# Layer 3 attention of a four-layer kernel: fp32 probabilities against values in four column tiles of the array, and row maxima taken bank by bank

## The reference, cut to what matters

```python
q = (q_input @ W_Q + b_Q)      # q_input is the layer norm of x: 16 x 56 x 128
k = (kv_input @ W_K + b_K)     # kv_input is ctx_1024: 16 x 1500 x 128
v = (kv_input @ W_V + b_V)
sim = einsum('bhqd,bhkd->bhqk', q, k) / sqrt(8)      # 16 heads of 8
sim = where(mask, finfo.min, sim)
attn = softmax(sim, axis=-1)
out = einsum('bhqk,bhkd->bhqd', attn, v)             # heads joined again
return out @ W_O + b_O
```

## Time and profile before

| | us |
|---|---|
| median of three executions | 1914.12 |
| lowest, highest | 1910.27, 1917.18 |
| profiled execution | 1911.53 |
| its span (first to last instruction) | 1909.8 |
| layer 3 attention, steady part of the span | 1222 to 1747 |

### The profile page before, as it was taken

The page is one execution under the profiler, slowest core; times in us unless marked ns, Lnnn a source line. Parts: engine busy times, 40 slices in busy tenths (PEclk is TensorE's granted clock), DMA queues, the critical chain, the costliest instruction groups (busy, mean ns, idle before and its releaser), DMA issues. The chain is left out here.

```text
span 1909.8 us, 31074 instructions
## 1 busy us (share of the span) xinstructions
PE 1628.9 (85%) x10638; PEld 1374.8 (72%) x10638; DVE 1356.4 (71%) x2304; ACT 932.8 (49%) x1353; POOL 706.8 (37%) x613
## 2 busy tenths in 40 slices
PE   3995686637999999999999957799999999996796
PEld 2994375436999999999999823577777777774795
DVE  5214544675888888888888633688888888883598
ACT  1331222224666666666666404466666666662332
POOL 0110000003333334334333001587877787873230
PEclk8897798668999999999999978799999999998798
DMA  2014496101111111111110001425344353520110
GB/s 54 23 44 112 115 237 118 33 1 33 34 59 40 32 32 48 49 32 32 32 56 8 3 3 49 112 68 118 80 100 98 84 114 81 115 54 3 56 45 21
DMA packets 97600, 116.02 MB, mean 61 GB/s; under 512 B 16785, under 2 KB 82882, under 8 KB 97538
## 3 DMA queue, kind: packets, MB, share of 16 engines
q1 hardware_dynamic: 97538, 115.23, 24.5%
HBM read 76.42 MB, written 0.46 MB: 40 GB/s over the span
## 5 line engine op out<-in xcount | busy, mean ns | idle before, releaser
L2295 POOL TENSOR_TENSOR l3att_PL<-l3att_P,l3att_PH 125x1120 fp32r<-125x1120 f32 x128 | 329.9, 2577 | 121.8 <-DVE l3att_PH L2376 61.3
L1728 ACT CAST l2att_PT<-PS 125x512 fp32r<-125x512 f32 x336 | 175.3, 595 | 221.3 <-PE PS L1667 221.3
L1768 DVE TENSOR_REDUCE l2att_neg<-PS 128x1 f32<-128x1500 f32 x112 | 192.7, 1720 | 76.8 <-PE PS L1660 76.8
L2197 ACT ACTIVATE l3att_P<-PS 125x1344 f32<-125x1344 f32 x128 | 165.4, 1292 | 136.9 <-PE PS L2077 134.9
L1774 DVE TENSOR_TENSOR l2att_PT<-PS,l2att_PT 125x512 fp32r<-125x512 f32 x336 | 210.1, 680 | 1.5 <-ACT l2att_PT L1728 1.5
L1667 PEld LDWEIGHTS PS<-all_ident,l_P 128*125 128x125 f32 x1344 | 163.5, 187 | 15.0 <-DVE l_P L1782 6.5
L1737 ACT ACTIVATE l_P<-PS,l2att_neg 128x1500 f32<-128x1500 f32 x112 | 171.0, 1527 | 3.9 <-DVE l2att_neg L1768 3.9
L1699 PE MATMUL PS<-l2att_PT,l_cc 125*128 125x256 f32 x576 | 170.5, 296 | 0.0
L1667 PE MATMUL PS<-all_ident,l_P 128*125 128x128 f32 x1344 | 165.4, 273 | 4.8 <-DVE l_P L1782 4.8
L1701 PE MATMUL PS<-l2att_PT,l_cc 125*128 125x256 f32 x576 | 162.5, 282 | 0.0
L1703 PE MATMUL PS<-l2att_PT,l_cc 125*128 125x256 f32 x576 | 162.4, 282 | 0.0
(11 more groups left out here) (526 smaller groups left out, 3755.3 us busy)
## 6 DMA issues: line engine op xcount, KB each, us to landing
l3att_KS<-l3att_kh SPq DMA_DIRECT2D x128, 187.5 KB, 4.0
l_QP<-in_ctxT SPq DMA_DIRECT2D x8, 1500.0 KB, 11.2
l_cT<-in_ctxT SPq DMA_DIRECT2D x16, 750.0 KB
l_c<-in_ctx SPq DMA_DIRECT2D x16, 750.0 KB
l3att_cT<-in_ctxT SPq DMA_DIRECT2D x16, 750.0 KB, 4.8
l3att_KS<-l3att_kl SPq DMA_DIRECT2D x64, 187.5 KB, 3.8
l_QP<-in_ctx SPq DMA_DIRECT2D x8, 1344.0 KB
l0f_w<-in_L_ffn_W SPq DMA_DIRECT2D x16, 256.0 KB, 3.1
```

What stands on the lines that cost most here:

```text
L1728: act.copy(PT[:, 4 * g:4 * g + 4, PLACE[u1], 0, :], PS[0:CHUNK, 3 * s1 + g, :].rearrange("k (c r) -> k c r", r=128)).then_inc(hi_in, 1)
L1768: v.tensor_reduce(neg[:, s:s + 1], E, XY_AXES, ALU.max, negate=True).then_inc(top_in, 1)
L2197: act.activation(P[s][:, PART * part:PART * part + PART, :].rearrange("p (i j) r -> p i (j r)", j=2), PS[0:CHUNK, 3:6, 0:2 * SET_ROWS], AC ...
L2295: g.tensor_tensor(PL[s][:, part, :, :], P[s][:, PART * part:PART * part + SPLIT, :], PH[s][:, part, :, :], ALU.subtract).then_inc(pl_in, 1)
```

## The change

The change is confined to layer 3's attention.

- `P` is no longer split. The casts to `PH`, the subtractions to `PL`, the fp32 copy `VF` of the values and their low part are gone. The values `VS` are fp32 with 9 columns for each head (`VCOLS` = 9: 8 features and a one).
- `values` issues, for each of 12 chunks, four fp32 matmuls, one for each head: weights 125 x 9, streamed 125 x 56, written to PSUM partitions 32h to 32h+8 of columns 0 to 55. Each head thus has its own 32 columns of the array. The blocks of four other pairs of heads are not computed.
- ACT copies the 128 x 56 result straight into `OC` (`outputs`). `OB` and the 64 extraction DMAs are gone. `OC`, `WOS`, `SEL` and `inv` have 128 partitions. DVE clears the 56 columns of banks 6 and 7 once at the start.
- The maxima are taken by the bank: six `tensor_reduce` of 500 keys for each group in place of two of 1500. The six row matmuls go to banks 0, 2, 0, 2, 0, 1 (`PLACES`), each waits for the maximum that read its bank before, and each raises `sr_ps`. Two small `tensor_reduce` (minimum over three) write `negs` and `negm` in place of the cast.
- The keys' projection and the matmul with `SEL` move from bank 2 to bank 1 (`SIDE`), the former to before `rows(2)`. The order on the PE becomes: rows 0 and 1, `values` of chunks 0 to 3, `maxima`, `project_keys`, the matmul with `SEL`, row 2, `project_values`, row 3, `turned(0)`, rows 4 and 5, `values` of chunks 4 to 11, `turned(1)`. ACT writes keys and values first, then exponential, output copy, exponential. DVE's list becomes: maxima 0 and 1, copy into `QB`, maximum 2, low keys, inverse, maxima 3 to 5, scaling of `OC`, the two minima, the subtraction.

The diff, cut to its core:

```diff
-VCOLS = 17
+VCOLS = 9
-SPLIT = PART - 1
+QUAD = 32
...
-            VS = [self.sb(ctx, f"VS{s}", [CHUNK, CHUNKS, SETS, SETS * VCOLS], F32R) for s in range(2)]
+            VS = [self.sb(ctx, f"VS{s}", [CHUNK, CHUNKS, SETS, SETS, VCOLS]) for s in range(2)]
...
-            PH, PL = ([self.sb(ctx, f"{n}{s}", [CHUNK, 2, SPLIT, SET_ROWS], F32R) for s in range(2)]
-                      for n in ("PH", "PL"))
...
-                            pe.wait_ge(vl_in, (n - 2) // SETS * BANKS + BANKS)
-                        parts = 1 if chunks[0] < PART else 2
-                        pe.wait_ge(pl_in, 2 * n - 4 + parts)
...
+                            if k % PART == 0 or k == chunks[0]:
+                                pe.wait_ge(p_in, 2 * n - 3 + k // PART)
+                            for h in range(SETS):
+                                mm = pe.matmul(PS[QUAD * h:QUAD * h + VCOLS, 6 + u % 2, 0:TOK],
+                                               VS[s][:, k, a, h, :], P[u % 2][:, k, TOK * h:TOK * h + TOK],
+                                               start=k == 0, stop=k == CHUNKS - 1)
...
+                    if now:
+                        rows((0, 1))
+                    if before:
                         values((0, 1, 2, 3))
...
+                    if now:
+                        rows((2,))
...
+                    if now:
+                        rows((3,))
+                    if then:
+                        turned(0)
+                    if now:
+                        rows((4, 5))
+                    if before:
+                        values((4, 5, 6, 7, 8, 9, 10, 11))
+                    if then:
+                        turned(1)
...
-                    def high_part():
-                        act.wait_ge(p_in, 2 * n - 1)
-                        act.copy(PH[s][:, 0, :, :], P[s][:, 0:SPLIT, :]).then_inc(ph_in, 1)
...
-                        act.copy(OB[:, a % SETS, :], PS[0:SETS * VCOLS, 6 + u % 2, 0:SET_ROWS]
+                        act.copy(OC[:, bass.ds((n - 2) // SETS, 1), a, :], PS[:, 6 + u % 2, 0:TOK].unsqueeze(1)
                                  ).then_inc(o_in, 1)
...
-                        for part in range(2):
-                            g.wait_ge(ph_in, 2 * n - 1 + part)
-                            g.tensor_tensor(PL[s][:, part, :, :], P[s][:, PART * part:PART * part + SPLIT, :],
-                                            PH[s][:, part, :, :], ALU.subtract).then_inc(pl_in, 1)
...
+                            v.tensor_reduce(parts[:, u % 2, half, i:i + 1], PS[0:HROWS, PLACES[p], 0:BANK_KEYS],
+                                            X_AXIS, ALU.max, negate=True).then_inc(top_in, 1)
...
-                        v.tensor_copy(negs[:, u % 2, :, 1], negm[:, u % 2, :]).then_inc(nh_in, 1)
-                        v.wait_ge(nh_in, n + 1)
+                        v.tensor_reduce(negs[:, u % 2, :, 1], parts[:, u % 2, :, :], X_AXIS, ALU.min)
+                        v.tensor_reduce(negm[:, u % 2, :], parts[:, u % 2, :, :], X_AXIS, ALU.min
+                                        ).then_inc(hi_in, 1)
+                        v.wait_ge(hi_in, n + 1)
...
-                        v.tensor_copy(PH[s][:, 1, :, :], P[s][:, PART:PART + SPLIT, :]).then_inc(ph_in, 1)
```

More of the change, by code:

```diff
@@ L1876, in attend_sets @@
         HROWS = SET_ROWS // 2
-        ROWS17 = SETS * VCOLS
+        PLACES = (0, 2, 0, 2, 0, 1)
+        SIDE = 1
         with ExitStack() as ctx:
@@ new lines, in one, with rows @@
+                    g, more = u % SETS, known is None or known < GROUPS - SETS
+                    late = g == 1 and (known is None or SETS < known < GROUPS)
+                    weighs = g == SETS - 1 and live(known, 2 * SETS - 1, GROUPS)
+                    def rows(places):
+                        s = u // SETS
+                        for p in places:
+                            half, i = p // BANKS, p % BANKS
+                            if p == 0:
+                                pe.wait_ge(ks_in[s][g], n // UNROLL * 48 + 48)
+                                if g == 0:
+                                    pe.wait_ge(mask_in[s], n // UNROLL * 16 + 16)
+                                if known == 0:
+                                    pe.wait_ge(ones_in, 64)
+                                pe.wait_ge(qb_in, n + 1)
+                                if known != 0:
+                                    pe.wait_ge(top_in, 6 * n - 1)
+                            elif 2 <= p <= 4:
+                                pe.wait_ge(top_in, 6 * n + p - 1)
+                            elif p == 5:
+                                if known is None or known >= 1:
+                                    pe.wait_ge(top_in, 6 * n)
+                                if g < BANKS and more:
+                                    pe.wait_ge(kl_in, b * BANKS + BANKS + g + 1)
+                                if weighs:
+                                    pe.wait_ge(inv_in, n // SETS)
+                            pe.matmul(PS[0:HROWS, PLACES[p], 0:BANK_KEYS],
+                                      QB[s][0:97, g, HROWS * half:HROWS * half + HROWS],
+                                      KS[s][0:97, g, BANK_KEYS * i:BANK_KEYS * i + BANK_KEYS],
+                                      start=True, stop=True).then_inc(sr_ps, 1)
@@ L2114, in values @@
+                        if chunks[-1] == CHUNKS - 1:
                             mm.then_inc(o_ps, 1)
-                    if live(known, 2, GROUPS):
+                    now, then, before = live(known, 0, GROUPS), live(known, 1, GROUPS), live(known, 2, GROUPS)
+                    if now:
+                        rows((0, 1))
+                    if before:
                         values((0, 1, 2, 3))
-                    if live(known, 1, GROUPS):
+                    if then:
                         maxima()
-                    if live(known, 0, GROUPS):
-                        rows(0)
@@ L2268, in block_queries @@
                         BM[:, :].unsqueeze(2).to_broadcast([96, SETS, TOK]), ALU.mult).then_inc(qb_in, 1)
-                for i in range(BANKS):
-                    low_values(0, 0, i)
-                g.wait_ge(vl_in, BANKS)
                 for n in range(2 * SETS):
```

226 lines of the change are left out of this document (79 added, 147 removed).

## The result

The changed kernel takes 1829.24 us (median of 4 runs, 1817.16 to 1833.05) against 1913.88 us of the kernel before on the same chip: a ratio of 0.9544, 95% interval 0.9522 to 0.9566, so 84.6 us less. The forecast was 136 us less. The profiled execution took 1828.54 us, its span is 1826.8 us against 1909.8 before.

| stretch | before | after | difference | forecast |
|---|---|---|---|---|
| start to the first maximum | 1203.5 | 1201.5 | -2.0 | 0 |
| first maximum of group 0 to that of group 63 | 524.1 | 458.6 | -65.5 | -130 |
| from there to the end of the attention | 28.0 | 16.1 | -11.9 | -6 |
| joining of the sets behind it | 14.2 | 10.1 | -4.1 | 0 |
| span | 1909.8 | 1826.8 | -83.0 | -136 |

The account below looks back on a forecast made before the run. DVE was taken to bound: 5.95 us of work plus 0.3 of waits, a 6.25 us period. 63 x (8.32 - 6.25) = 130 plus 6 at the end, 136 off: 1778 against the median; range 1756 to 1878.

Parts of the forecast that it names:

- two tiles: Value matmuls on PE: only two column tiles run at a time, period 7.15 us, 1832 us; chance 25%.
- a stall that is not POOL's: DVE's cast: its small operation still costs 1.2 us without POOL's load, 1836 us; chance 5%.
- Four tiles side by side: Value matmuls on PE: four column tiles overlap, 0.094 us a chunk, 1.13 us for 12.
- Array changes: PE switching the array from whole to quarters and back, twice a group: 0.096 us each, four 0.38 us.
- DVE's sizes: DVE operations per group: a maximum of 500 values 0.673 us, each of two minima 0.157, all work 5.95.
- the extraction's wait: End of the attention: the sums' matmul waited 5.64 us for the last extraction DMA; this was to go.
- 63 x (8.32 - 6.25) = 130 us: Attention groups: the period from group to group falls from 8.32 to 6.25 us, 130 us less over 63 periods.
- the PE is fed: Value records and loads on PE are fed slowly or run serially: 0.375 us per chunk, 1971 us; chance 18%.
- What is late next: Waits between PE and DVE: the next group's row 0 late by a few tenths; 0.3 us of waits taken.
- The sum for the PE: PE work per group: 4.15 kept, 1.13 values, 0.38 array changes, 5.66 us in all.
- DVE the bound: Attention period: DVE's 5.95 us of work sets it, 6.25 us with waits; forecast held at 52%.
- 6 us at the end: End of the attention: extraction wait gone and shorter drain of the last two groups, 6 us, between 5 and 9.

Follow-up runs that it names:

- experiment 4: Kernel before with the cast of the negated maxima into negs replaced by a minimum over one element: 1914.2 us, ratio 0.9992.
- experiment 3: Kernel before with only the value part of the change, 1909.38 us; the same with the PE's loop written out, 1878.92 us.

## Why the prediction was right, and where it was not

The time measured, 1829.24 us, lies within the forecast range, 1756 to 1878, and on the forecast side; the likeliest value, 1778, was 51 us too low. It lies outside the forecast's own range, 1756 to 1800. Only the rivals with two tiles (1832) and with a stall that is not POOL's (1836) had carried the range so far, and neither came true: the trace shows four tiles and a free subtraction. So that 1829 lies within it, beside 1832, is luck.

**Right.**
- Four tiles side by side: 0.098 us a chunk against 0.094; 12 chunks 1.18 us against 1.13. The rule of the Trainium skill weighed there ("TensorE: Matmul & The Clock Gate", Part 3), that a load overlaps matmuls in flight only where its row group differs, does not hold here: 6144 loads with the same 125 rows were busy for 81.3 us beside the matmuls. By an estimate from the Trainium skill, "TensorEngine Tiling (Array Packing)", Instruction Overhead, a chunk would have taken 0.20 us; here it is half of that.
- Array changes: 0.1 us each (the last row starts at 1456.95 and takes 0.23 to the next start, the values begin at 1457.28).
- DVE's sizes: 0.669 us the median reduction against 0.673; minima 0.15 to 0.16 against 0.157; and the small subtraction at 0.16 in place of a stalled cast. The stall was POOL's, as said, but it falls on the subtraction too once the cast no longer takes it (experiment 4).
- POOL and ACT do not bound, the extraction's wait is gone.

**Wrong: the step "63 x (8.32 - 6.25) = 130 us".** The period was 7.28, 63 x 1.03 = 65 us more than forecast. Of its own signs of being right, the 6.25 us from start to start, the 6.9 us in the step with the inverse, DVE busy for over 90% and the PE waiting for DVE more than the reverse all failed. The miss has three causes, sized by the sums over the groups, 458.6, 426.3 and 403.1:

1. *The jump of the PE's loop*, 458.6 - 426.3 = 32.3 us, 29.7 of them at the jumps. The prediction has no term for it. It took no notice that the values went from 22 instructions of the code to 48 per group, and the body of the loop from 832 matmuls and loads to 1984. Nothing in the trace before showed a price for it; the rival "the PE is fed" had named streams of small records as the danger, and the place turned out to be another.
2. *The first step of a batch*, 426.3 - 403.1 = 23.2 us. ACT's key copy waits for DMAs out of the only key tile. "What is late next" had been looked for only between PE and DVE. In the trace before, with steps of 7.9 to 8.7 us, no key copy waited for a DMA; a shorter period has less room for it, and the wait grows as the rest gets faster (24.6 us in the kernel after, 39.1 written out).
3. *Means over four steps*, 403.1 - 63 x 6.25 = 9.4 us. The sum for the PE put keys and projection at three quarters each in every group. But they are not spread evenly: two steps of four hold both, and their PE work is rows 1.37, turned 1.31, values 1.18, changes 0.38, maxima 0.20, keys 0.85 and projection 0.87 = 6.16 us, with some 0.5 us of waits for ACT's copies and exponentials: 6.67. "DVE the bound" holds for one step of four, 6.46. DVE was busy for 74%, not over 90%, and also two neighbouring reductions overlap by 0.08 us, so that its own sum was lower than thought.

**Wrong: the step "6 us at the end".** It gained 12 in the drain and 4 in the joining of the sets behind it. Last rows of the attention in the kernel after, answering to the earlier trace rows:

```profile
1672.31 0.78 PE L2095 MATMUL PS<-l3att_P,l3att_VS 125*9 125x56 f32 x48 [0.67 <-ACT l3att_P L2180]
1673.15 0.21 ACT L2188 COPY l_OC<-PS 128x56 f32<-128x56 f32 x1 [0.90 <-PE PS L2095]
1673.41 0.65 PE L2114 MATMUL PS<-l_OC,l3att_SEL 128*128 128x224 f32 x2 [0.33 <-ACT l_OC L2188]
```

The sums' matmul waits 0.33 us for a copy in place of 5.64 for a DMA. The drain without casts and subtractions gave some 6.6 us more, which had been put at under 1 and at most at 3.4. The joining then runs partly at the full clock: before, all of it lay behind the idle time and at the lower level, 1.2 GHz. Its 16 matmuls with `W_O` start 0.75 us apart before; after, the first seven do so too, and from 1681.91 us on, with the clock back at 2.4 GHz from 1681.7, they start 0.37 apart. That saves 3.2 us, and what follows the start of the last one takes 1.93 us in place of 2.80.

Taken together: 65 us too much for the groups, 12 us too little for the rest (2 of them scatter ahead of the first maximum), 53 net.

## What to carry to other kernels

Add up an engine's work for each kind of step, not for their mean: the step that holds everything sets the period, and the light one doesn't pay it back. When a change makes many small instructions of few, look at what loops they lie in, as a jump in a long body can cost several us and the clock behind it, and writing the loop out shows it at once. A stalled small operation on DVE beside a busy POOL is cured by taking POOL's work away, not by another operation in its place if the next one stalls in its turn; and matmuls in separate columns of the array need an order in which neighbours go to different ones.

## What the runs showed of the hardware that was not expected

- A jump back in a PE loop of 1984 matmuls and loads leaves the PE idle for 4.7 to 5.0 us and costs 5.9 us in all; one of 832 costs nothing that can be seen. Instruction packets come all through the long loop (55 between 1330 and 1670 us) and not at all in the short one. The written-out code has about as many as a loop (43 and 49 in the kernels of experiment 3), so the packets alone don't make the gap.
- The records of fp32 matmuls of 9 x 56 in four column tiles start 6 to 7 ns apart, and the eight records of four matmuls with their eight loads take 0.098 us. In an order that stays in one tile for 8 records they take 0.24 us, for 16 records 0.32.
- An operation on DVE of only 224 numbers with two SBUF inputs takes 2.27 us beside POOL's subtractions, 0.16 without; a reduction of the same size takes 0.15 to 0.16 in both cases.
